# Units 0 to 5 pair their last two tiles in the out-projection's memory; later row sums; another order in the last unit and in centring

## The reference

```python
x = x + cross_attention(layernorm(x), context)      # its own layer norms of both sides inside
x = x + linear(layernorm(x), fp6 blocks of 32)      # weights and inputs rounded to an fp6 grid
# cross_attention: 16 heads of 32, q = xn @ Wq.T, k = cn @ Wk.T, v = cn @ Wv.T
# scores = q k / sqrt(32), masked; attn = softmax(scores); out = (attn @ v) @ Wo.T + bo
```

## Time and profile before

| what | before |
|---|---|
| median of three runs | 4507.2 us |
| the profiled execution | 4507.71 us |
| its span, first to last instruction | 4505.9 us |
| mean granted clock of PE | 0.993 of full speed |
| busy: PE | 4345.9 us (96%) |
| busy: DVE, ACT, POOL | 3443.6, 2814.4, 2718.9 us (76%, 62%, 60%) |

### The profile page before, as it was taken

How to read it: one execution, slowest core, us unless ns; L and a number is a source line. 1 busy time by engine, 2 the same in 40 slices (tenths; PEclk the granted TensorE clock), 3 DMA queues, 4 the chain that set the end, 5 groups by cost and what they waited for, 6 DMA issues and landing times.

```text
span 4505.9 us, 89640 instructions
## 1 busy us (share of the span) xinstructions
PE 4345.9 (96%) x36880; PEld 1506.5 (33%) x36880; DVE 3443.6 (76%) x4023; ACT 2814.4 (62%) x5128; POOL 2718.9 (60%) x1706
## 2 busy tenths in 40 slices
PE   4999999999999999999999999999999999999999
PEld 2322343223432234322343223422234222342223
DVE  5788667886678866888668886688866888668885
ACT  3387734877447864478645785458754587546784
POOL 2288552885428854388544885348853588525884
PEclk9999999999999999999999999999999999999999
DMA  5355642557326573356633556335663365543654
GB/s 191 73 118 118 150 136 61 120 118 180 109 59 123 114 192 99 68 117 121 177 100 69 119 120 175 102 77 116 123 167 106 75 123 115 167 111 74 123 113 108
DMA packets 190012, 532.35 MB, mean 118 GB/s; under 512 B 28625, under 2 KB 102673, under 8 KB 148386
## 3 DMA queue, kind: packets, MB, share of 16 engines
q0 software_dynamic: 43776, 318.79, 35.3%
q1 hardware_dynamic: 145826, 207.83, 15.0%
HBM read 110.98 MB, written 21.01 MB: 29 GB/s over the span
## 4 chain that ended last, share of the span: by engine, by line
PE 73%; DVE 12%; DMA 5%; ACT 4%; issue 3%; POOL 2%; SPq 0%; DVEq 0%; ACTq 0%; POOLq 0%
PE banks L1048 20%; PE banks L1060 17%; PE banks L956 16%; PE banks L1016 12%; PE banks L1091 5%; DVE max_parts L621 5%; DMA wdT<-wkT_wvT_wqT 3%; ACT region L835 2%; PE banks L925 2%; DMA sums<-wkT_wvT_wqT 2%; PE banks L950 1%; DVE amax L569 1%; DVE x_stats L536 1%; DVE region L759 1%; DVE qscale L571 1%
## 5 line engine op out<-in xcount | busy, mean ns | idle before, releaser
L621 DVE TENSOR_REDUCE max_parts<-banks 128x2 f32<-128x1024 f32 x2048 | 2402.1, 1218 | 454.3 <-PE banks L1016 442.4
L835 ACT ACTIVATE region<-banks 128x512 f32<-128x512 f32 x4096 | 2191.1, 616 | 506.2 <-PE banks L1048 401.1
L427 POOL TENSOR_TENSOR wkT_wvT_wqT<-region 128x1024 f32<-128x1024 f32 x528 | 1284.7, 2518 | 668.0 <-ACT region L835 662.6
L1048 PE MATMUL banks<-queries_stacked,keys_stacked 98*32 98x512 f16 x16384 | 1317.7, 384 | 21.6 <-ACT values L822 7.1
L1060 PE MATMUL banks<-region,values 128*32 128x512 f32 x8192 | 1076.8, 600 | 12.3 <-ACT region L835 9.2
L1048 PEld LDWEIGHTS banks<-queries_stacked,keys_stacked 98*32 98x32 f16 x16384 | 415.5, 95 | 1149.3 <-ACT region L835 842.0
L1016 PE MATMUL banks<-keys_stacked,queries_stacked 33*128 33x512 f16 x4096 | 701.5, 386 | 7.2 <-DVE max_parts L621 3.5
L956 PE MATMUL banks<-region,wkT_wvT_wqT 128*128 128x512 f16 x2304 | 557.3, 381 | 12.6 <-DMA wkT_wvT_wqT<-weights_split 10.3
L427 POOL TENSOR_TENSOR sums<-region 128x1024 f32<-128x1024 f32 x144 | 358.8, 2617 | 92.1 <-ACT region L835 91.8
L956 PE MATMUL banks<-wkT_wvT_wqT,region 128*128 128x512 f16 x1536 | 368.8, 380 | 0.0
L1016 PEld LDWEIGHTS banks<-keys_stacked,queries_stacked 33*128 33x128 f16 x4096 | 180.2, 93 | 559.4 <-issue 352.2
(11 more groups left out here) (92 smaller groups left out, 3224.0 us busy)
## 6 DMA issues: line engine op xcount, KB each, us to landing
wdT<-wkT_wvT_wqT POOLq DMA_DIRECT2D x96, 1024.0 KB, 11.7
wkT_wvT_wqT<-wkT_wvT_wqT POOLq DMA_DIRECT2D x80, 1024.0 KB, 7.3
sums<-wkT_wvT_wqT POOLq DMA_DIRECT2D x72, 1024.0 KB, 7.3
wkT_wvT_wqT<-sums POOLq DMA_DIRECT2D x40, 1024.0 KB, 7.2
region<-in_x SPq DMA_DIRECT2D x24, 1024.0 KB, 8.9
wkT_wvT_wqT<-weights_split SPq DMA_DIRECT2D x8, 3072.0 KB, 19.0
keys_stacked<-region SPq DMA_DIRECT2D x384, 64.0 KB, 2.0
keys_stacked<-sums SPq DMA_DIRECT2D x384, 64.0 KB, 2.0
```

Of the source, the lines that this page charges most:

```text
L427: e.tensor_tensor(SUMS[dst][:, half], PR[i][:, half], PR[i + 1][:, half], ALU.add).then_inc(s_pr, 1)
L621: e.tensor_reduce(mpart[:, buf, :, a, t, c], MXB[parity], AX.X, ALU.max).then_inc(s_mxd, 1)
L835: e.activation(PR[u % 4][:, j * HALF:j * HALF + HALF], score_bank(m % NU, kt, j)[0], ACT.Exp, scale=SCALE).then_inc(s_ex, 1)
L1048: mm = e.matmul(dst[HD * t:HD * t + HD, :], KA[0:STR, ds(ka + (j * C + (u + 1) * P + HD * t), HD)], QA[0:STR, ds(qa[j], HALF)], start=True ...
```

## The change

1. **Pairing.** In units 0 to 5 POOL makes an eighth pair, tiles 14 and 15, into a new buffer SUMS[5], which is the memory of the out-projection weights (WO). It stands behind pair 6 on POOL. ACT's exponentials of tiles 2 and 3 of units 1 to 6 wait for its halves. PE no longer sums PR[2] and PR[3] for these units; it sums SUMS[5] once. WO is loaded for every batch, by SP during unit 6, and not once at the start.
2. **Row sums** of the unit before stand in steps 3, 4 and 5 (the change's words count tiles, 4 to 6): the first buffer, SUMS[5], SUMS[4]. Bank 7 is cleared in step 3. So tiles 0 to 3 of units 1 to 6, and tiles 0 to 7 of unit 0, rotate their scores over three banks.
3. **Last unit.** SUMS[4] is summed in step 8 and not in step 5; the copy of the row sums moves from tile 7 to tile 10. DVE makes pair 4 before the inverse, and it and tiles 10 to 13 go into the buffer "one", after the first merge out of it has landed. The FFN weights' load stands before SP's last wait of the unit.
4. **Centring.** The next batch's x tokens: DVE keeps the statistics (chunk 0 at tiles 1 and 2 of the tail, chunk 1 behind tile 8), POOL makes the reciprocal deviation and minus the mean times it (`next_rstd`), ACT does the centring (`centred`).

```diff
-    NEXT_AT = (2, 6)
+    NEXT_AT = (2, T // P - 1)
-            [sb("sums3", [P, J * HALF], F32)[:, :], WD[:, :, :].rearrange("p c d -> p (c d)")]
+            [sb("sums3", [P, J * HALF], F32)[:, :]] + [w_[:, :, :].rearrange("p c d -> p (c d)") for w_ in (WD, WO)]
...
+            if n == 0 and tile < 8:
+                slot = 4 * tile + j + 1
+                return bank((7, 4, 5)[slot % 3]), 3 if slot > 3 else None
+            if tile < 4:
+                return bank((7, 4, 5)[(4 * tile + j) % 3]), 3
             if tile < 8 or n == NU - 2:
-                return bank(4 + j % 2), 2
+                return bank(4 + j % 2), 3 if tile == 4 and j < 2 else 2
...
-            e.dma_start(WO[:, :, :], woT.rearrange("(c p) n -> p c n", p=P)).then_inc(s_w, 16)
...
+                        if 2 * g + q == NU - 1:
+                            e.wait_ge(s_pv, (b * NU + NU - 2) * KT + 4 + 5)
+                            e.dma_start(WO[:, :, :], woT.rearrange("(c p) n -> p c n", p=P)).then_inc(s_wo, 16)
...
+                e.dma_start(SUMS[4], wd_dram).then_inc(s_fl, 16)
                 e.wait_ge(s_pv, b * (NU * KT) + NU * KT + 4)
-                e.dma_start(SUMS[4], wd_dram).then_inc(s_fl, 16)
...
+                def next_rstd(c):
+                    e.wait_ge(s_ve, call_next(b, NEXT_AT[c]))
+                    e.wait_ge(s_nx, (b + 1) * NCH + c)
+                    e.tensor_tensor(rs[:, :], ve[:, :], mhalf[:, :], ALU.pow).then_inc(s_nr, 1)
+                    e.wait_ge(s_nr, 2 * (b * XCH + c) + 1)
+                    e.tensor_tensor(nb[:, :], mv[:, :, 0], rs[:, :], ALU.mult).then_inc(s_nr, 1)
+                    e.wait_ge(s_nr, 2 * (b * XCH + c) + 2)
+                    e.tensor_scalar(nb[:, :], nb[:, :], -1.0, None, ALU.mult).then_inc(s_rs, 1)
...
-                        e.wait_ge(s_pv, n * KT + 4 + 3)
+                        e.wait_ge(s_pv, n * KT + 4 + (3 if g + q == 0 else 4))
...
                         pair(6, two)
+                        if 2 * g + q < NU - 2:
+                            if g + q > 0:
+                                e.wait_ge(s_pv, n * KT + 4 + 5)
+                            elif b > 0:
+                                e.wait_ge(s_op, b * TT)
+                            for h in range(2):
+                                half = ds(2 * HALF * h, 2 * HALF)
+                                e.wait_ge(s_ex, n * (KT * J) + 15 * J + 2 * h + 4)
+                                e.tensor_tensor(SUMS[5][:, half], PR[2][:, half], PR[3][:, half],
+                                                ALU.add).then_inc(s_pt, 1)
...
-                                ins = e.tensor_tensor(SUMS[second][:, half], SUMS[second][:, half], PR[t % 4][:, half],
+                                ins = e.tensor_tensor(SUMS[one][:, half], SUMS[one][:, half], PR[t % 4][:, half],
...
                         pair(3, three)
+                        e.wait_ge(s_acc, (3 * m + 1) * 16)
+                        pair(4, one)
                         invert_first(m - 1)
                         invert_rest()
                         normalise(m - 1, n - 1)
-                        e.wait_ge(s_pv, m * KT + 4 + 6)
-                        pair(4, second)
...
+                def centred(c, first, n):
+                    e.wait_ge(s_rs, call_next(b, NEXT_AT[c]))
+                    for i in range(first, first + n):
+                        ins = e.activation(chunk_tokens(c)[:, i, :], chunk_tokens(c)[:, i, :], ACT.Identity,
+                                           bias=nb[:, i:i + 1], scale=rs[:, i:i + 1])
...
-                    e.wait_ge(s_pv, m * KT + kt + (2 if kt in (2, 3) else 1))
+                    e.wait_ge(s_pv, m * KT + kt + (2 if kt in (2, 3) and n in (0, NU - 1) else 1))
+                        if j % 2 == 0 and kt in (2, 3) and 0 < n < NU - 1:
+                            e.wait_ge(s_pt, 2 * (b * (NU - 2) + n - 1) + j // 2 + 1)
...
+                            if n > 0:
+                                if end and t == 0:
                                     sums = [(PR[3], None)]
-                                if t == 2:
-                                    sums = [(SUMS[buffers(2 * g + q - 1)[0]], (s_acc, 48 * m))]
-                                if t == 5:
-                                    sums = [(SUMS[4], (s_ac2, 16 * (b * (2 * NU - 2) + 2 * (2 * g + q))))]
+                                if t == (2 if end else 3):
+                                    sums = [(SUMS[buffers(n - 1)[0]], (s_acc, 48 * m))]
+                                if t == 3 and not end:
+                                    fresh = (s_ex, ex + 4 * J + 2)
+                                if t == 4 and not end:
+                                    sums = [(SUMS[5], (s_pt, 2 * (b * (NU - 2) + n)))]
+                                if t == closing:
+                                    sums = [(SUMS[4], (s_ac2, 16 * (b * (2 * NU - 2) + 2 * n)))]
...
-                        left = [(PR[2], None)]
+                        left = [(PR[2], None)] if n == NU - 2 else ()
```

More of the change, by code:

```diff
@@ L412, in low_tokens @@
                             rstd(call)
+                        if cc == 1 and halfway:
+                            halfway()
                 if b == 0:
@@ L551, in centre, with token_stats @@
                 return e.tensor_scalar(dst, src, mean, rstd, ALU.subtract, ALU.mult)
+            def token_stats(c, b, call):
+                e.wait_ge(s_x[c % 3], b * (NCH // 3 * 16) + c // 3 * 16 + 16)
+                if c >= XCH:
+                    e.wait_ge(s_rs, call - 1)
+                yield from norm_stats([chunk_tokens(c)[:, i, :] for i in range(4)], stats, mv, ve[:, :], c < XCH)
             def norm(c, b, call):
@@ L555, in norm @@
                 twice = c < XCH
-                e.wait_ge(s_x[c % 3], b * (NCH // 3 * 16) + c // 3 * 16 + 16)
-                yield from norm_stats(tiles, stats, mv, ve[:, :], twice)
+                yield from token_stats(c, b, call)
                 yield
@@ L752, in _ @@
                 unit(G - 1, 1, True)
-                parts = queries_tokens(b + 1, [call_next(b, i) for i in NEXT_AT]) if b + 1 < B else iter(())
+                parts = [token_stats(c, b + 1, call_next(b, NEXT_AT[c])) if b + 1 < B else iter(()) for c in range(XCH)]
                 def x1_tile(i):
@@ L783, in _ @@
                         x1_tile(i)
+                    if i == TT + 1:
+                        for _ in parts[1]:
+                            pass
                     if i >= 3:
                         y_tile(i - 3)
-                    if i >= 1:
-                        next(parts, None)
+                    if 1 <= i <= NEXT_AT[0]:
+                        next(parts[0], None)
         @blk.scalar
@@ L861, in unit @@
                             halfway = None
-                            if kt == 7 and n > 0:
+                            if kt == 7 and 0 < n < NU - 1:
                                 halfway = lambda: row_sums(m - 1, KT + 6)
+                            if kt == 10 and end:
+                                halfway = lambda: row_sums(m - 1, KT + 9)
                             if kt == 10 and not end:
@@ L1036, in score @@
                                 e.wait_ge(s_ex, ex + (u + 1) * J + j + 3 - back)
-                            elif tile == 9:
+                            elif n == NU - 2 and tile == 9:
                                 e.wait_ge(s_mxd, (b + 1) * NH + 1)
-                            else:
+                            elif n > 0:
                                 e.wait_ge(s_mxd, (b + 1) * NH + 2)
@@ L1072, in step @@
                         mm = outputs()
-                        if end:
+                        if end and sums:
                             mm.then_inc(s_po, 1)
@@ L1121, in turn_next @@
                         turn_maxima(m + 1, 1 - q)
+                    closing = 8 if end else 5
                     def quad(k, ex, ka, v, rows):
@@ L1153, in unit @@
                     if end:
-                        left = [(PR[3], None), (second, (s_pr, m * 14 + 16)), (first, (s_acc, 48 * (m + 1)))]
+                        left = [(PR[3], None), (one, (s_pr, m * 14 + 16)), (first, (s_acc, 48 * (m + 1)))]
                     else:
-                        left = [(PR[2], None)]
+                        left = [(PR[2], None)] if n == NU - 2 else ()
                     nqa = None if end else [((2 * ng + nq) * (J * HALF) + j * HALF) for j in range(J)]
```

41 lines of the change are left out of this document (28 added, 13 removed).

## The result

| | median us | runs | range |
|---|---|---|---|
| before | 4506.39 | 4 | 4500.99 to 4507.52 |
| after | 4433.58 | 4 | 4432.94 to 4435.58 |

The ratio is 0.9841, with a 95% interval of 0.9825 to 0.9856: 72.8 us less, where 66 were forecast (4441). The profiled execution took 4433.29 us, its span 4431.5. The total came out nearly as said, but made up otherwise. The table cuts each of the eight batches at the same matmuls and shows the means in us: the front begins with its first projection matmul (L956 before, L1022 after), a unit with its first weighted values, the tail with the first out-projection matmul; the tail ends where the next batch's front begins. What lies ahead of the first front (64.99 before, 65.94 after) and behind the last tail (3.22 and 4.61) is in no column.

What follows compares the result with a forecast made beforehand. PE was taken to bound units 0 to 6, with POOL next. 57 us there, 5 in the last unit and 4 from centring make 66 off 4507.7: 4441 us, own range 4425 to 4460, 8 in 10 4416 to 4480.

Steps and rivals of the forecast that it cites:

- PE in units 0 to 6: Inner units: fewer row sums and a third score bank change PE's steps by -1.37, to 43.4 us a unit.
- the next in line: Inner units: POOL, with the eighth pair at 4.67, needs 43.5 us alone, 43.75 with `merge_last`'s wait.
- Rival A: Inner units: the eighth pair costs 5.34, so POOL sets a pace of 44.4; 4479 in all; chance 0.22.
- its cover: Inner units: POOL's idle time of 6.0 us, said to be used up to 0.3.
- Rival C: Inner units: POOL's adds lengthen the late merge's landing, so `merge_last` holds POOL; 4547 at 15.2; chance 0.05.
- Unit 0: First unit of a batch: the edge, step 14 and six two-bank steps at 0.15 give -1.8 us.
- Unit 6: POOL ends last there, starting 1.3 later behind PE and losing waits of 0.4: +0.9 us.
- The last unit: The wait for SUMS[4] goes, merges' landings into the first buffer come next; -0.65 us a batch, -5 in all.
- Centring: Tails: 0.6 saved at tile 6 in seven tails, DVE's centring free elsewhere; -4 us in all.
- Waits that cost nothing: Pair 2's wait, the unit's end told by `s_pv`, SUMS[4]'s sum in step 5, WO's load: each at 0.
- The front: Start of a batch, ahead of unit 0's first weighted values: no term, predicted change 0.
- Its signs: Inner units 43.4 to 43.8 would show it, above 44.3 wrong; POOL's first adds 1.6 to 3 behind step 0.

Runs made afterwards that it cites:

- e4: Changed kernel with DVE taking the maxima of the next unit's tile 0 ahead of the inversion of the row sums: 4414.09 us, 0.9787 of before.
- e8: e4 with the eighth pair's two adds on POOL cut to half their columns: 4409.77 us, 0.9782 of before.
- e2: Changed kernel with the eighth pair's adds on POOL cut to half their columns: 4435.39 us.
- e10: The same code as e4, run again: 4414.6 us, 0.9793 of before.
- e3: Changed kernel with the scores of tiles 0 to 7 rotating over two banks as before: 4468.5 us.
- e7: Changed kernel with parts 1 and 2 taken back (no eighth pair, old row-sum steps, two banks), parts 3 and 4 kept: 4485.21 us, 0.995 of before.
- e5: Changed kernel with part 3, the last unit's edits, taken back: 4436.85 us, 0.9842 of before.
- e1: Changed kernel with DVE's inversion of the row sums in units 1 to 5 replaced by a reciprocal of two columns: 4412.1 us.
- e6: Changed kernel with part 4 taken back, the centring on DVE again: 4448.94 us, 0.9872 of before.

## Why the prediction came out, point by point

- **PE in units 0 to 6: the size failed, in one step.** "Step 0, 3.40 to 2.52 [...]; step 1, 2.66 to 2.52": in units 2 to 5 they became 2.91 and 2.85. The other steps that the sum names came as forecast: edge 2.74 (2.8), step 2 2.51 (2.6), step 3 3.48 (3.4), step 4 3.39 (3.3), step 14 2.47 (2.52). Step 5, which it left out, went from 3.25 to 3.41. Without DVE's inversion in the way PE's unit is 43.53 (e4, e8) for the 43.4 predicted. The step that failed is "the next in line": I asked of POOL what is late next and gave it a sum; for DVE I read its 39.18 of 44.80 and no more, though what counted was its load inside two steps, 1.66 us of inversion. This cost 0.7 in each of units 2 to 5, 22 us in all.
- **POOL, the next in line: right in its sizes, wrong in its rank.** 4.65 by starts for the 4.67 taken; `merge_last` waits 0.30 in the unit shown and 0.31 in the median of 56, for the 0.25 taken. It isn't far behind PE: its first add stands 1.22 behind step 0 in unit 3, as before (1.3), not 1.6 to 3. By the prediction's own numbers its cover was 5.97 - 4.67 - 1.37, which is nothing, and not the 0.3 it states. But halving its new work changed nothing, with DVE in the way (e2) or without (e8). Rival A's premise, that the pair may cost 5.34, took a printed duration that overlaps its neighbour's for a cost. Rival C, a longer landing, did not come.
- **Unit 0: -1.8 predicted, -2.75 in the means.** Its shortest in each kernel are 42.62 and 40.51, -2.1. The rest is the clock: in batch 5 the first 3.84 us of the unit ran at a granted 0.60, behind waits of 0.78 and 0.35 for ACT, and in batch 4, behind the same two waits, they didn't (columns as in the first window above; the second row covers the same work and more):

```profile
2929.56:2933.40 3.84, 3.84 (x33) 0.92 (x33) 0.55 (x1) 2.01 (x4) 2.63 (x2) 0.60 0.00 0
```

```profile
2384.37:2388.00 3.63, 3.63 (x44) 1.02 (x44) 1.76 (x2) 3.10 (x6) 2.53 (x2) 1.00 0.00 0
```

  The matmuls that took 1.94 there instead of 1.03 are at 1.2 of 2.4 GHz. Such a unit is 1.4 longer. Three of the eight of the changed kernel have it; of before five are over 43.7, two of them near 45.9. It comes and goes from one run of a kernel to the next (unit 0 took 41.17 in e4 and 40.80 in e10, the same code). But over all traces such starts are 18 of 24 in the kernels that give unit 0's first scores two banks (before, e3, e7) and 26 of 72 in the others, so a part of it may belong to the change, by way of the shorter waits; no run shows this by itself.
- **Unit 6: +0.9 predicted, +0.43.** The direction was right, the reason, POOL's lag, for the most part not: with half of the pair's work gone the unit still took 42.62 (e2). DVE's inversion moved gave 0.21 (e4, 42.41), and POOL's work halved on top of it 0.23 (e8, 42.18, the time of before).
- **The last unit: mechanism right, -0.65 predicted, -0.8 by e5's cuts and -0.9 by e7's.** The wait for SUMS[4] went, the landing ends it in seven batches of eight. A new wait of 0.38 to 0.69 for ACT in seven of them, which the prediction hadn't, took a part back. Some 0.6 of the -1.46 isn't assigned; the mean of the last unit lies between 36.16 (e1) and 36.97 (e10) in kernels that all have part 3.
- **Centring: the step failed.** "DVE had waited for ACT anyway, so its centring was free": it was free of DVE's own time, but not of POOL's. 4 us were predicted and 15 found by e6. I read one tail, at tile 6, for a 0.6 that ran straight into the maxima, and didn't compare the distances between tiles 3, 4 and 5, which stood in the trace of before at 7.12 beside 6.69 for tiles 2 and 3.
- **Waits that cost nothing** cost nothing: e8 has all of them, and PE is busy for the whole of its inner unit. Line 1157 has 1664 matmuls, as said.
- **The front: left at nothing, 0.77 found.** The third bank for unit 0's first scores acts there too (e3). The prediction counted it from unit 0's first step only.
- **Its signs.** Inner units were to take 43.4 to 43.8 and took 44.25, just under the 44.3 that it called wrong.

So 21 us too much in units 2 to 5 stood against 8 too little in unit 0, 4 in unit 6, 6 in the last unit, 7 in the tails and 6 in the front; the stretches outside the table took 2.3 back. The total is only 7 off because these cancel, which is luck: its sign and size were right, and its reason for the inner units' pace was not.

## What to carry to other kernels

When matmuls go from a step, list what every other engine does in that step, not in the whole unit: an engine with 5 us of slack a unit can have none in the step that was shortened. Moving its rare work (here 1.66 us of inversion) to the steps that remain long cost nothing that the traces show and gave 19 us. An operation that fills an engine's idle time is free only if no neighbour on another engine slows beside it; compare repeated intervals of one loop with and without it before calling it free.

## What the runs showed of the hardware that I had not expected

- DVE's tensor_scalar over 128x512 fp32 and POOL's operations slow each other: POOL's small one 0.26 to 0.49, two of DVE's 0.99 to 1.95 (e6).
- DVE's tensor_scalar over 128x16 takes 0.17 alone; where one of POOL's adds over 128x512 runs beside it, it ends 0.03 to 0.04 after that add, 0.60 to 0.89 long (all 40 of the changed kernel), up to 1.11 in e6's tail shown above.
- The same two waits of PE, 0.78 and 0.35 long and 1.2 us apart, were followed by 3.8 us at a granted clock of 0.60 in batches 0, 5 and 6, and by full clock in the other five (changed kernel). Waits of 0.89 and 0.56 at that place were followed by a lower clock in five of eight batches of before and seven of eight of e3.
- POOL's printed durations of two adds (5.33) overlap the next instruction by some 0.67; starts give 4.66.
